# Feed-forward stage of an 8-core recurrent layer: hidden activations kept feature-major, quantized slice by slice without TensorE transposes

## The reference

```python
def simple_rms_norm(x, dim):
    rms = jnp.sqrt(jnp.mean(x * x, axis=-1, keepdims=True) + EPS_RMS)
    return x / rms * dim ** (-0.5)
def activation_quant(x):
    scale = 127.0 / jnp.clip(jnp.max(jnp.abs(x), axis=-1, keepdims=True), EPS_Q)
    return jnp.clip(jnp.round(x * scale), -128, 127) / scale
def weight_quant(w):
    return jnp.sign(w) * jnp.mean(jnp.abs(w))
def bit_linear(x, w, b, dim_in):
    x_q = activation_quant(simple_rms_norm(x, dim_in))
    return jnp.einsum('bsd,od->bso', x_q, weight_quant(w)) + b

xn = _layernorm(x, axis=-1)                 # x: (4, 2048, 2048)
s = recurrent_branch(xn)                    # LN'd input, scan, gate, Wo
h = bit_linear(xn, w1, b1, 2048)            # to 8192 features
g = silu(bit_linear(gelu(h), w2, b2, 8192)) # back to 2048
out = x + s * g
```

## Time and profile before

| what | us |
|---|---|
| median of 2 runs | 3588.7 (3581.41 and 3595.99) |
| the profiled execution, device time | 3576.5 |
| its span on the slowest core (core 0) | 3574.9 |
| spans of the eight cores | 3530.1 to 3574.9 |
| `_p6` with its tail, about | 1500 to 2227 |
| `_p7`, about | 2227 to 2891 |
| `_p8`, about | 2891 to 3575 |

### The profile page before, as it was taken

How to read it: one execution, slowest core, us unless ns; L and a number is a source line. 1 busy time by engine, 2 the same in 40 slices (tenths; PEclk the granted TensorE clock), 3 DMA queues, 4 the chain that set the end, 5 groups by cost and what they waited for, 6 DMA issues and landing times.

```text
span 3574.9 us, 24771 instructions; the slowest of 8 cores (3530.1 to 3574.9 us)
## 1 busy us (share of the span) xinstructions
PE 1823.3 (51%) x6888; PEld 701.2 (20%) x6888; DVE 1305.0 (37%) x1314; ACT 995.7 (28%) x1563; POOL 251.5 (7%) x80
## 2 busy tenths in 40 slices
PE   2212534444417657567777774111111139999963
PEld 1101200000003223222222221000000014444421
DVE  4565345555522212122222223334444403333345
ACT  3111055555511000022222222111111155455312
POOL 0000023333310000000000000010000000000000
PEclk9999955555559878788888887555555559999965
DMA  3100145555551231332223332222222254454325
GB/s 107 47 24 24 17 153 189 179 185 187 184 124 22 46 72 37 98 101 95 94 94 98 97 97 85 94 71 70 71 71 71 71 173 171 151 193 160 118 106 188
DMA packets 190400, 378.64 MB, mean 106 GB/s; under 512 B 79232, under 2 KB 130560, under 8 KB 167456
## 3 DMA queue, kind: packets, MB, share of 16 engines
q1 hardware_dynamic: 184032, 359.04, 30.4%
q0 software_dynamic: 6240, 18.02, 3.1%
HBM read 294.26 MB, written 100.66 MB: 110 GB/s over the span
## 4 chain that ended last, share of the span: by engine, by line
PE 42%; DMA 21%; DVE 18%; ACT 7%; issue 5%; another core or an unknown queue 3%; POOL 2%; SPq 1%; DVEq 0%; ACTq 0%; POOLq 0%
PE pmA L772 14%; PE pmA L936 14%; DMA p_w<-w1T 8%; DMA p_hg<-hgsc 5%; DMA p_s<-s1Tsc 5%; PE pmA L720 4%; PE pmA L684 3%; ACT p_s L595 3%; ACT p_k2x L881 2%; DVE p_t L861 2%; DVE p_t L868 2%; DVE p_k L872 2%; PE pmC L406 2%; POOL p_int L857 2%
## 5 line engine op out<-in xcount | busy, mean ns | idle before, releaser
L772 PE MATMUL pmA<-p_s,k1T 128*128 128x512 bf16 x2048 | 491.2, 400 | 213.2 <-DMA p_s<-s1Tsc 213.2
L936 PE MATMUL pmA<-p_k2g,p_s 128*128 128x512 bf16 x2048 | 494.6, 403 | 57.3 <-ACT p_s L925 57.3
L878 PE MATMUL pmC<-consts,p_k 128*128 128x128 bf16 x512 | 127.7, 267 | 550.4 <-DVE p_k L872 531.9
L772 PEld LDWEIGHTS pmA<-p_s,k1T 128*128 128x128 bf16 x2048 | 200.7, 101 | 503.5 <-issue 314.4
L936 PEld LDWEIGHTS pmA<-p_k2g,p_s 128*128 128x128 bf16 x2048 | 199.5, 101 | 352.1 <-issue 224.4
L881 ACT ACTIVATE p_k2x<-pmC 128x128 bf16<-128x128 bf16 x512 | 130.0, 278 | 468.4 <-PE pmC L878 459.4
L561 PE MATMUL pmA<-p_yp,Est_t 128*32 128x512 f32 x128 | 115.1, 1054 | 282.9 <-POOL p_yp L557 282.7
L780 DVE SCALAR_TENSOR_TENSOR p_h<-pmA,a1col,p_b1B 128x512 f32<-128x512 f32 x128 | 96.1, 751 | 408.3 <-PE pmA L772 408.3
L950 DVE TENSOR_TENSOR p_S<-p_S,pmA 128x1024 f32<-128x1024 f32 x112 | 136.8, 1221 | 289.9 <-PE pmA L936 289.9
L784 ACT ACTIVATE p_hg<-p_h 128x512 f32<-128x512 f32 x128 | 80.6, 629 | 487.8 <-DVE p_h L780 487.8
L861 DVE SCALAR_TENSOR_TENSOR p_t<-p_hg,a1col,p_int 128x8192 f32<-128x8192 f32 x8 | 70.0, 8751 | 385.8 <-POOL p_int L857 385.8
(11 more groups left out here) (144 smaller groups left out, 1867.3 us busy)
## 6 DMA issues: line engine op xcount, KB each, us to landing
p_w<-w1T SPq DMA_DIRECT2D x64, 1024.0 KB, 5.8
p_w<-w2T SPq DMA_DIRECT2D x64, 1024.0 KB, 5.2
s1Tsc<-p_s SPq DMA_DIRECT2D x64, 512.0 KB, 3.4
p_s<-s1Tsc SPq DMA_DIRECT2D x16, 2048.0 KB, 9.8
hgsc<-p_hg SPq DMA_DIRECT2D x128, 256.0 KB, 2.0
p_hg<-hgsc SPq DMA_DIRECT2D x8, 4096.0 KB, 24.9
p_xb<-x_sh SPq DMA_DIRECT2D x16, 1024.0 KB, 5.3
k2Tsc<-p_k2x SPq DMA_DIRECT2D x8, 2048.0 KB, 12.0
```

The lines of the kernel that those rows point to most:

```text
L772: bld.op(TE, lambda e, tt=tt, k=k, pb=pb, sb_=sb_: e.matmul(pb[:, 0:512], k1T[:, k * TOWN + tt * 128:k * TOWN + (tt + 1) * 128], sb_[:, k ...
L878: bld.op(TE, lambda e, k=k, pb=pb: e.transpose(pb, k2b[:, k * 128:(k + 1) * 128], consts[:]), reads=[(k2b, 0), consts], writes=[(pmC, f"C{ ...
L936: bld.op(TE, lambda e, ic=ic, ds=ds, tc=tc, pb=pb, kg=kg, s2b=s2b: e.matmul(pb[:, tc * 512:(tc + 1) * 512], s2b[:, ic * 2048 + ds * 128:ic ...
```

## The change

The hidden activations are produced with features on partitions and tokens along the free dimension, and stay so.

- The matmuls of `_p6` swap operands: a 128x128 block of signs is stationary, 512 tokens of `k1T` move. There are as many as before, of the same shape. A step is now a feature slice `ic` (64 of them, 4 in a slab), with two halves `tc` of 512 tokens.
- The token factor is now needed along the free dimension. Before the loop it is turned into a row by 8 small matmuls and broadcast to 128 partitions (`a1b`) by two more. VectorE multiplies PSUM by it; the bias `b1c`, now one column for a slice (32 KB in all), goes into ScalarE's Gelu. ScalarE squares to a tile; GpSimd adds the squares up (`acs`) and VectorE keeps their maximum (`acm`), each one pass of 128x1024 a slice. The hidden slice is written in one piece of 512 KB.
- After the loop the sum over partitions is taken by a matmul with ones, the maximum over partitions by a GpSimd `reduce_max` over 128x1024 along the partition axis. Eight operations on rows of 1x1024 give the factors; two matmuls broadcast `c2` to `c2b`, and 8 small ones turn the scale back into columns.
- After a barrier, quantization runs over 64 slices of 128x1024 in place of 8 tiles of 128x8192: load 512 KB, GpSimd multiply, ScalarE integer copy, four VectorE passes, write 256 KB. All tiles are double. The 512 transposes and their 512 copies are gone.

```diff
-    b1B_hbm = nc.dram_tensor("b1B", [128, INNER], F32, kind="ExternalInput").ap()
+    b1B_hbm = nc.dram_tensor("b1B", [128, 64], F32, kind="ExternalInput").ap()
...
-    hg_hbm = nc.dram_tensor("hgsc", [TOWN, INNER], F32, kind="Internal").ap()
+    hg_hbm = nc.dram_tensor("hgsc", [INNER, TOWN], F32, kind="Internal").ap()
...
-        _p7(nc, bld, dbg, debug, env)
...
+        bld.op(SY, lambda e: e.dma_start(out=b1c[:, 0:64], in_=b1c_hbm),
+               writes=[b1c], slot='b1B')
...
+            bld.op(TE, lambda e, tt=tt: e.matmul(
+                pmA[0:1, tt * 128:(tt + 1) * 128], a1col[:, tt:tt + 1],
+                eyef[:, 0:128], start=True, stop=True),
+                reads=[(a1col, "a1"), eyef], writes=[(pmA, bk)])
+        bld.op(VE, lambda e: e.tensor_copy(rows[0:1, 0 * TOWN:1 * TOWN], pmA[0:1, 0:TOWN]),
+               reads=[(pmA, "A0"), (pmA, "A1")], writes=[(rows, "a1r")])
+        for tc in range(2):
+            bk = f"A{tc}"
+            bld.op(TE, lambda e, tc=tc: e.matmul(
+                pm[tc][:, 0:512], onesf[0:1, 0:128],
+                rows[0:1, 0 * TOWN + tc * 512:0 * TOWN + (tc + 1) * 512], start=True, stop=True),
+                reads=[(rows, "a1r"), onesf], writes=[(pmA, bk)])
+            bld.op(VE, lambda e, tc=tc: e.tensor_copy(
+                a1b[:, tc * 512:(tc + 1) * 512], pm[tc][:, 0:512]),
+                reads=[(pmA, bk)], writes=[(a1b, 0)])
...
+            for oc in range(16):
+                sb_ = ssl2[oc % 2]
+                bld.op(SY, lambda e, oc=oc, sb_=sb_: e.dma_start(
+                    out=sb_.rearrange("p (k c) -> p k c", k=16),
+                    in_=s1T_hbm[:, oc * 512:(oc + 1) * 512].rearrange("(k p) c -> p k c", p=128)),
+                    reads=[(L["s1T_hbm"], 4 * kq + oc // 4) for kq in range(16)],
...
+                for icl in range(4):
+                    ic = oc * 4 + icl
+                    hgc = hgc2[ic % 2]
+                    h2b = h2b2[ic % 2]
+                    for tc in range(2):
+                        bi = (2 * ic + tc) % 3
+                        pb = pm[bi]
+                        for k in range(16):
+                            bld.op(TE, lambda e, k=k, icl=icl, tc=tc, pb=pb, sb_=sb_: e.matmul(
+                                pb[:, 0:512],
+                                sb_[:, k * 512 + icl * 128:k * 512 + (icl + 1) * 128],
+                                k1T[:, k * TOWN + tc * 512:k * TOWN + (tc + 1) * 512],
+                                start=(k == 0), stop=(k == 15)),
+                                reads=[(sb_, 0)] + k1rd, writes=[(pmA, f"A{bi}")],
+                                inc=(1 if k == 15 else 0))
+                        h1 = h1b2[tc]
+                        bld.op(VE, lambda e, pb=pb, h1=h1, tc=tc: e.tensor_mul(
+                            h1[:], pb[:, 0:512], a1b[:, tc * 512:(tc + 1) * 512]),
+                            reads=[(pmA, f"A{bi}"), (a1b, 0)], writes=[(h1b2[tc], 0)])
+                        bld.op(SC, lambda e, h1=h1, hgc=hgc, tc=tc, ic=ic: e.activation(
+                            out=hgc[:, tc * 512:(tc + 1) * 512], in_=h1[:], func=AF.Gelu,
+                            bias=b1c[:, ic:ic + 1]),
+                            reads=[(h1b2[tc], 0), b1c], writes=[(hgc, tc)])
+                        bld.op(SC, lambda e, hgc=hgc, h2b=h2b, tc=tc: e.activation(
+                            out=h2b[:, tc * 512:(tc + 1) * 512],
+                            in_=hgc[:, tc * 512:(tc + 1) * 512], func=AF.Square),
+                            reads=[(hgc, tc)], writes=[(h2b, tc)])
+                    if ic == 0:
+                        bld.op(GP, lambda e, h2b=h2b: e.tensor_copy(acs[:], h2b[:]),
+                               reads=[(h2b, 0), (h2b, 1)], writes=[(acs, 0)])
+                        bld.op(VE, lambda e, h2b=h2b: e.tensor_copy(acm[:], h2b[:]),
+                               reads=[(h2b, 0), (h2b, 1)], writes=[(acm, 0)])
+                    else:
+                        bld.op(GP, lambda e, h2b=h2b: e.tensor_add(acs[:], acs[:], h2b[:]),
+                               reads=[(h2b, 0), (h2b, 1), (acs, 0)], writes=[(acs, 0)])
+                        bld.op(VE, lambda e, h2b=h2b: e.tensor_max(acm[:], acm[:], h2b[:]),
+                               reads=[(h2b, 0), (h2b, 1), (acm, 0)], writes=[(acm, 0)])
+                    bld.op(SY, lambda e, hgc=hgc, ic=ic: e.dma_start(
+                        out=hg_hbm[ic * 128:(ic + 1) * 128, :], in_=hgc[:]),
+                        reads=[(hgc, 0), (hgc, 1)], writes=[(hg_hbm, ic)],
+                        slot=f'hgw{ic % 2}')
...
+        for tc in range(2):
+            bk = f"A{tc}"
+            bld.op(TE, lambda e, tc=tc: e.matmul(
+                pm[tc][0:1, 0:512], onesf[:, 0:1],
+                acs[:, tc * 512:(tc + 1) * 512], start=True, stop=True),
+                reads=[(acs, 0), onesf], writes=[(pmA, bk)])
+            bld.op(VE, lambda e, tc=tc: e.tensor_copy(
+                rows[0:1, 1 * TOWN + tc * 512:1 * TOWN + (tc + 1) * 512],
+                pm[tc][0:1, 0:512]),
+                reads=[(pmA, bk)], writes=[(rows, "sq")])
+        bld.op(GP, lambda e: e.reduce_max(
+            out=rows[0:1, 2 * TOWN:3 * TOWN], in_=acm[:], axis=AX.C),
+            reads=[(acm, 0)], writes=[(rows, "mx2")])
+        bld.op(SC, lambda e: e.activation(
+            out=rows[0:1, 3 * TOWN:4 * TOWN], in_=rows[0:1, 1 * TOWN:2 * TOWN], func=AF.Sqrt,
+            bias=epsc[0:1, 1:2], scale=epsc[0:1, 2:3]),
+            reads=[(rows, "sq"), epsc], writes=[(rows, "rms2")])
+        bld.op(SC, lambda e: e.activation(
+            out=rows[0:1, 4 * TOWN:5 * TOWN], in_=rows[0:1, 2 * TOWN:3 * TOWN], func=AF.Sqrt),
+            reads=[(rows, "mx2")], writes=[(rows, "mxa")])
...
+        bld.op(VE, lambda e: e.reciprocal(out=rows[0:1, 5 * TOWN:6 * TOWN], in_=rows[0:1, 5 * TOWN:6 * TOWN]),
+               reads=[(rows, "iden2")], writes=[(rows, "iden2")])
+        bld.op(VE, lambda e: e.tensor_mul(rows[0:1, 6 * TOWN:7 * TOWN], rows[0:1, 4 * TOWN:5 * TOWN],
+                                          rows[0:1, 5 * TOWN:6 * TOWN]),
+               reads=[(rows, "mxa"), (rows, "iden2")], writes=[(rows, "mm2")])
...
+        for tc in range(2):
+            bk = f"A{tc}"
+            bld.op(TE, lambda e, tc=tc: e.matmul(
+                pm[tc][:, 0:512], onesf[0:1, 0:128],
+                rows[0:1, 7 * TOWN + tc * 512:7 * TOWN + (tc + 1) * 512], start=True, stop=True),
+                reads=[(rows, "c2r"), onesf], writes=[(pmA, bk)])
+            bld.op(VE, lambda e, tc=tc: e.tensor_copy(
+                c2b[:, tc * 512:(tc + 1) * 512], pm[tc][:, 0:512]),
+                reads=[(pmA, bk)], writes=[(c2b, 0)])
...
+            bld.op(TE, lambda e, tt=tt: e.matmul(
+                pmB[:, tt:tt + 1], rows[0:1, 6 * TOWN + tt * 128:(6 * TOWN + (tt + 1) * 128)],
+                onesf[0:1, 0:1], start=True, stop=True),
+                reads=[(rows, "mm2"), onesf], writes=[(pmB, "B0")])
+        bld.op(VE, lambda e: e.tensor_copy(a1col[:, 8:16], pmB[:, 0:8]),
+               reads=[(pmB, "B0")],
+               writes=[(a1col, f"mm2_{tt}") for tt in range(8)])
+        bld.cut()
...
+            for ic in range(64):
+                hgb, vb = hgb2[ic % 2], vb2[ic % 2]
+                intb, tb, k2c = intb2[ic % 2], tb2[ic % 2], k2c2[ic % 2]
+                bld.op(SY, lambda e, ic=ic, hgb=hgb: e.dma_start(
+                    out=hgb[:], in_=hg_hbm[ic * 128:(ic + 1) * 128, :]),
+                    reads=[(hg_hbm, ic)], writes=[(hgb, 0)], slot=f'hgr{ic % 2}')
...
+                bld.op(GP, lambda e, hgb=hgb, vb=vb: e.tensor_mul(
+                    vb[:], hgb[:], c2b[:]),
+                    reads=[(hgb, 0), (c2b, 0)], writes=[(vb, 0)])
+                bld.op(SC, lambda e, vb=vb, intb=intb: e.activation(
+                    out=intb[:], in_=vb[:], func=AF.Copy, bias=256.50002),
+                    reads=[(vb, 0)], writes=[(intb, 0)])
+                bld.op(VE, lambda e, vb=vb, intb=intb, tb=tb: e.tensor_sub(
+                    tb[:], vb[:], intb[:]),
+                    reads=[(vb, 0), (intb, 0)], writes=[(tb, 0)])
+                bld.op(VE, lambda e, tb=tb, k2c=k2c: e.tensor_scalar(
+                    out=k2c[:], in0=tb[:], scalar1=-256.5, scalar2=None, op0=ALU.is_gt),
+                    reads=[(tb, 0)], writes=[(k2c, 0)])
+                bld.op(VE, lambda e, tb=tb, k2c=k2c: e.scalar_tensor_tensor(
+                    out=tb[:], in0=tb[:], scalar=-255.5, in1=k2c[:],
+                    op0=ALU.is_gt, op1=ALU.add),
+                    reads=[(tb, 0), (k2c, 0)], writes=[(tb, 0)])
+                bld.op(VE, lambda e, tb=tb, intb=intb, k2c=k2c: e.scalar_tensor_tensor(
+                    out=k2c[:], in0=tb[:], scalar=257.0, in1=intb[:],
+                    op0=ALU.subtract, op1=ALU.add),
+                    reads=[(tb, 0), (intb, 0)], writes=[(k2c, 0)])
+                bld.op(SY, lambda e, ic=ic, k2c=k2c: e.dma_start(
```

(44 more changed lines are left out.)

167 lines of the change are left out of this document (26 added, 141 removed).

## The result

| | us |
|---|---|
| before, median of 10 runs | 3573.1 |
| after, median of 11 runs | 3783.2 |
| ratio after/before, 95% interval | 1.0587 [1.0554, 1.0621] |
| forecast | 3852, range 3775 to 3925 |

The account below looks back on a forecast made before the run. It took exposed waits to bound the kernel: slab loads behind writes, and quantization as a sum of latencies. Quantization +160, between stages +102, first-layer loop +1 gave +263 us; from the 3588.7 median, 3852, range 3775 to 3925.

Parts of the forecast that it names:

- Quantization, +160 forecast: Quantization stage: 64 serial slices of 12.8 us, 823 us with last write and barrier, against 663.3 before.
- The step it rests on: Quantization: SP queues each load behind the previous slice's write, so second buffers go unused and a slice costs all its latencies.
- The rival of working double buffers: Quantization: loads pass ahead, a slice costs VectorE's 4.9 us, stage 324, kernel 3352 us; chance 0.03.
- Between the stages, +102 forecast: From last Square to quantization: 126.4 us with the GpSimd maximum and what follows, against 24.3 before.
- The maximum over partitions: Between the stages: GpSimd passes 128 partitions' elements one after another at L857's 0.866 ns, 113.5 us.
- the rival of a cheap reduction: Between the stages: the maximum costs about one pass, 2.35 us; kernel 3741 us; chance 0.12 with serial slices.
- The estimate of 124 us: Between the stages: half the Trainium skill page's 247.7 us for [128, 2048]; would put the forecast 10 us later.
- What hangs on the reduction: Between the stages, after the maximum: row operations 5.7 us, broadcast, scale-column copy and barrier 3.2, with handovers 10.3 us.
- First-layer loop, +1 forecast: First-layer loop: slab loads behind larger writes +13 us, first slab without the bias load -11.5, sum +1.
- The bias load: First-layer start: the 4 MB load ahead of the first slab goes, its wait falling from 21.3 to 9.8 us, -11.5.
- The 0.9 us a slab: First-layer loop: each of 15 slab loads comes 0.9 us later behind a 512 KB write instead of 256, +13 us.
- Second layer, 0 forecast: Second layer: same matmuls and loads; TensorE already at granted clock 0.50 through quantization, so no slower start: 0 us.

Follow-up runs that it names:

- experiment 1: Changed kernel with the load of slice ic+2 queued ahead of the write of slice ic in quantization; 3404.0 us, ratio 0.953 to the kernel before.
- experiment 4: Changed kernel without VectorE's running maximum in the first-layer loop (only the first slice's kept); GpSimd's add back at 2.35 us; one run, 3797.6 us.
- experiments 5: Changed kernel with quantization over 32 pairs of slices, same serial order on SP; 3677.9 us, ratio 1.031 to the kernel before.
- experiment 10: Changed kernel with the load of slab oc+1 queued ahead of the writes of slab oc in the first-layer loop; 3551.8 us, ratio 0.997 to the kernel before.
- 6: Changed kernel with slices loaded ahead, slabs loaded ahead and the maximum over partitions by TensorE; 3100.5 us, ratio 0.868 to the kernel before.
- 7: Kernel before with only the order on SP changed, slab and token-tile loads queued ahead of writes; 3056.3 us, ratio 0.855 to the kernel before.

## Why the prediction was right

*Quantization, +160 forecast, +161.4 measured.* A slice was forecast at 12.8 us and is 826.2/64 = 12.9. The terms, in the order of the sum: load 3.7 forecast, 3.6 measured; GpSimd 2.35 and 2.34; ScalarE 1.11 and 1.06; VectorE 4.71 and 4.70 (2318.47 to 2323.17). The step it rests on, that SP holds the next load behind the write, was shown by experiment 1: only the place of the load in the queue was moved, and 392 us of the stage went. The rival of working double buffers was wrong for this kernel and right about its price in direction: with the loads ahead the stage takes 435 us (experiment 1), not the rival's 324, because the two engines that then overlap slow each other. (The whole, 3404 us against its 3352, compares less well, as the reduction in it was also priced too high.)

*Between the stages, +102 forecast, +69.6 measured: two terms mis-sized, in opposite directions.* (The last add took 3.39 instead of 2.35, for the reason of experiment 4.) The maximum over partitions was put at 113.5 us, 128 lanes one after another; it took 62.5. In L857's terms (0.866 ns a column) that is about half of the serial price; whether some lanes go in parallel or each element passes faster, one shape doesn't tell. But it is 27 times a plain pass: the rival of a cheap reduction (2.35 us) falls. The estimate of 124 us from the page of the Trainium skill ("GPSIMD Engine Reference", section 3.2), by half the columns, is twice too high for this shape; whether its 247.7 us hold for 2048 columns no run here shows. What hangs on the reduction was put at 10.3 us and took 27.8 (2269.88 to 2297.65): two reciprocals at 6.54 instead of one at 1.22 (the other was to be hidden, and the held-back scalar operation kept it from that), and eight small float32 matmuls for the scale column, about 6 us with their weight loads (0.5 us for two), which weren't counted. Without this second miss the kernel would have come out near 3766, just under the range: that its time lies inside, 8 us above the lower end, owes something to luck.

*First-layer loop, +1 forecast, -15 measured.* The bias load gave its 11; the other 4 can't be told from the spread of the cores and executions. The 0.9 us a slab for a larger write in front of it (13 us in all) didn't come: the median landing of a slab lay at 9.7 to 11.0 us on the cores of the kernel before and at 9.7 to 10.8 on those of the kernel after, and the write of 512 KB landed in 2.6 us, not 3.4.

*Second layer, 0 forecast, -11.4 measured.* Two cores of the profiled execution of before took 683 to 684 us there and the other six 646 to 650; after, all take 644 to 648. In experiments 5 and 10 two cores stood out in the same way (681 to 703 us), with nothing changed in that stage, so it doesn't belong to the change. The traces show what it is: on those two cores of before the 2048 matmuls are busy 495 us where core 6 has 460, with the same idle time ahead of them (57 and 54), and the granted clock over the dense stretch from 3020 to 3400 is 0.92 on average where core 6 has 1.00. That is 35 us on two of eight cores, 9 of the 11.4. The slowest core of that execution is one of the two. What lowers the clock there stays open.

The exposure of the slab loads was named in the forecast but not priced, since the change left it as it was; my expectations for 6 and 7 priced it 60 and 77 us too low, for the reason that experiment 10 shows.
